# Attention over 16 images: three PSUM banks in one ring for the short products, one bank for the long ones

## The chip, the cores and the metric

The kernel runs on one core of a Trainium2 chip. The metric is the device time of one execution in microseconds (us). Five engines work side by side, each in the order of its own program, and wait for each other through semaphores: PE (TensorE, matrix products; its weight loads are listed as PEld), DVE (VectorE), ACT (ScalarE), POOL (GpSimd) and SP (SyncE, which starts the DMAs). Products land in PSUM, which has eight banks of 128 partitions x 512 floats.

## The reference, cut to what matters

```python
x = x + mamba_block(layernorm(x), ...)          # x: (16, 224, 512)
qh = split_heads(layernorm(x) @ Wq + bq)        # 16 heads of depth 32
kh = split_heads(ctx @ Wk + bk)                 # ctx: (16, 750, 512)
vh = split_heads(ctx @ Wv + bv)
logits = einsum('bhqd,bhkd->bhqk', qh, kh) / sqrt(32) + mask * -1e9
out = einsum('bhqk,bhkd->bhqd', softmax(logits), vh)
x = x + merge_heads(out) @ Wo + bo
x = x + (gelu(layernorm(x) @ sign(w1).T * alpha1 + b1)) @ sign(w2).T * alpha2 + b2
```

The second addition is the phase that the change touches.

## The kernel before, in words

Three phases follow each other: the scan (functions up to line 995, which also makes keys and values for the attention), the attention (`attention_phase`, line 998) and the feed-forward part (from about line 1690). The order of all work is written out by hand, as a loop over slots for each engine.

In the attention each image b has 16 slots. The 224 queries are two tiles of 112 rows; the 16 heads are four groups g of four heads; G = 4b + g counts groups over all images. A slot is half of the 750 keys for one tile of queries and one group. With `at` = slot - 16b, what stands in a slot on PE, in this order, is:

- `scores(n)` (line 1164): four products into the four banks of `sps`. They wait until DVE has read the four products of the slot before.
- `transpose_p(m, pair)` for m = slot - 3 and pair = 0, 1, 2 (line 1180): four transpositions each of exponentials into a bank of `tps`. I call them the first, second and third tile of the slot. ACT copies the first and the third to `pT` (line 1315), DVE the second (line 1434).
- then, in some slots, one or two of these: `project_q` (line 1150, at = -2, 1, 5, 9), `transpose_h` twice (line 1131, at = -3, which is slot 13 of the image before), `out_proj` (line 1214, in slots 6 and 7 of the next image), `weigh_v` in two halves (line 1204, in slots 3 and 4, 7 and 8, 11 and 12, 15 and 16) and `spread_sums` (line 1189, in slots 4, 8, 12 and 16). A slot 16 is slot 0 of the next image. Slots 2 and 10 have nothing behind the transpositions.

On DVE a slot is: `scale_o` in every fourth slot (line 1453, it reads a weighed product), four reductions of the scores (line 1420), in slot 10 `stats_of_x1` for the next image (line 1383), `invert_sums` every fourth slot, in slot 8 `row_stats`, in slot 11 `normalise`, then the copy of the second tile (line 1434), then `add_residual` (line 1459, reads an output projection). On ACT a slot is: a copy of a query, of `transpose_h` or of the sums, if there is one, then an exponential (line 1307), the copy of the first tile, an exponential, the copy of the third tile.

Two sets of two banks hold what PE makes besides the scores. `tps` takes the tiles in turn: tile number % 2, three tiles a slot. `ups` takes everything else in turn, by a counter in `take_bank`. Before PE writes into a bank it waits for the semaphore that says that the last content has been read. `pt_act` and `pt_dve` count the copies of tiles, `q32`, `hT`, `rb`, `oT` and `x2` the readings of the others.

Of the kernel before, what the change touches and what calls it, by code (L numbers as in the profile page):

```python
# [7 lines left out]
P = 128  # L8
# [5 lines left out]
BANK = 512  # L14
# [983 lines left out]
def attention_phase(nc, t, x1_dram, x2_dram, k_dram, v_dram, mv_dram, mv2, row_mv, wsum, ident, shared, early, sps):  # L998
# [11 lines left out]

    B, D, KEYS = t["ctxT"].shape
    L = x1_dram.shape[1]
# [11 lines left out]
    SCALE = float(DH) ** -0.5  # L1025
    N_ALL = B * SLOTS
    assert KC * CHUNKS == KEYS and CHUNKS % 2 == 0 and 2 * L <= BANK

    pe, act, dve, pool, sp = nc.tensor, nc.scalar, nc.vector, nc.gpsimd, nc.sync
    with ExitStack() as stack:  # L1030
# [65 lines left out]

        def pairs_of(tile):
            return tile // PAIRS, tile % PAIRS

        def place(m, pair):  # L1100
# [4 lines left out]
        def transposed(tile):  # L1105
            return tps[0:KC, tile % 2, 0:4 * TT].rearrange("p (c l) -> p c l", c=4)

        def tensor_program():
            freed = [None, None]
            count = [0]  # L1110

            def take_bank(unit, sem, value):

                bank = bank_of[unit] = count[0] % 2
                count[0] += 1
                if freed[bank] is not None:
                    pe.wait_ge(*freed[bank])
                freed[bank] = (S[sem], value)
                return bank
# [6 lines left out]
            def transpose_h(b, part):  # L1126
                bank = take_bank(("hT", b, part), "hT", 2 * (b - 1) + part + 1)
                pe.wait_ge(S["ln"], b)
                for k2 in range(2):
                    for i in range(2):  # L1130
                        mm = pe.transpose(ups[:, bank, k2 * L + i * TT:k2 * L + (i + 1) * TT],
                                          ln[:, i, (2 * part + k2) * P:(2 * part + k2 + 1) * P], ident[0:TT, 0:TT])
                signal(("hT", b, part), mm)

            def value_bias():

                bank = take_bank("bv", "bo", 1)
                pe.wait_ge(S["bv"], 1)
                for k in range(KD):
                    mm = pe.matmul(ups[0:TT, bank, :], bv_wide[:, k, :], wo[:, k, :],  # L1140
                                   start=(k == 0), stop=(k == KD - 1))
                signal("bv", mm)

            def project_q(b, g):
                G = b * GROUPS + g
                bank = take_bank(("q", G, 0), "q32", G + 1)
                if b:
                    pe.wait_ge(S["hT"], 2 * b)
                for k in range(KD):
                    mm = pe.matmul(ups[:, bank, 0:L], wq[:, k, g * P:(g + 1) * P], hT[:, k, :],  # L1150
                                   start=(k == 0), stop=(k == KD - 1))
                signal(("q", G, 0), mm)
# [15 lines left out]
            def transpose_p(m, pair):  # L1168

                tile = m * PAIRS + pair  # L1170
                pe.wait_ge(S["exp"], 2 * m + (1 if pair == 0 else 2))
                if tile >= 2:
                    n, before = pairs_of(tile - 2)
                    if before == 1:
                        pe.wait_ge(S["pt_dve"], n + 1)
                    else:
                        pe.wait_ge(S["pt_act"], 2 * n + before // 2 + 1)
                for c in range(4):
                    head, chunk = divmod(4 * pair + c, CHUNKS)
                    mm = pe.transpose(tps[0:KC, tile % 2, c * TT:(c + 1) * TT],  # L1180
                                      sc[buffer_of(m // 2)][:, 2 * (m % 2) + head, chunk * KC:(chunk + 1) * KC],
                                      ident[0:TT, 0:TT])
                mm.then_inc(S["t_ps"], 1)

            def spread_sums(G):
                bank = take_bank(("r", G, 0), "rb", G + 1)
                pe.wait_ge(S["rwide"], G + 1)
                for i in range(2):
                    mm = pe.matmul(ups[:, bank, i * TT:(i + 1) * TT], rwide[:, i].rearrange("p j d -> p (j d)"),
                                   ident[0:TT, 0:TT], start=True, stop=True)  # L1190
                signal(("r", G, 0), mm)

            def weigh_v(b, g, part):
                G = b * GROUPS + g
                if part == 0:
                    take_bank(("pv", G, 0), "oT", G + 1)
                    pe.wait_ge(S["pt_act"], 2 * GROUP * (G + 1))
                    pe.wait_ge(S["pt_dve"], GROUP * (G + 1))
                    if b:
                        pe.wait_ge(S[f"v{b % 2}"], 16 * loads(b))  # L1200
                bank = bank_of["pv", G, 0]
                for c in range(part * CHUNKS // 2, (part + 1) * CHUNKS // 2):
                    for j in range(GROUP):
                        mm = pe.matmul(ups[j * DH:(j + 1) * DH, bank, 0:L],
                                       v[b % 2][:, c, (g * GROUP + j) * DH:(g * GROUP + j + 1) * DH],
# [4 lines left out]
            def out_proj(b, i):  # L1210
                bank = take_bank(("o", b, i), "x2", 2 * b + i + 1)
                pe.wait_ge(S["oT"], GROUPS * (b + 1))
                for g in range(GROUPS):
                    mm = pe.matmul(ups[0:TT, bank, :], oT[b % 2][:, g, i * TT:(i + 1) * TT], wo[:, g, :],
                                   start=(g == 0), stop=(g == GROUPS - 1))
                signal(("o", b, i), mm)

            def spread_alpha():
# [3 lines left out]
                for k in range(KD):  # L1222
                    mm = pe.matmul(ups[:, bank, k * P:(k + 1) * P], ones[:], diag[:, k, :], start=True, stop=True)
                signal("alpha", mm)

            def transpose_rows(k):
                bank = take_bank(("rows", k), "rows_lo", k + 1)
                pe.wait_ge(S["rows"], 1)
                for i in range(4):
                    mm = pe.transpose(ups[:, bank, i * P:(i + 1) * P], rows[:, i, k * P:(k + 1) * P], ident[:])  # L1230
                signal(("rows", k), mm)
# [11 lines left out]
            for slot in slots:  # L1243
# [10 lines left out]
                for b in range(B):  # L1254
# [21 lines left out]
        def scalar_program():  # L1276

            def keep_hT(b, part):
                act.wait_ge(S["unit"], unit_of["hT", b, part])
                act.wait_ge(S["unit"], unit_of["q", b * GROUPS - 1, 0])  # L1280
                act.activation(hT[:, 2 * part:2 * part + 2, :],
                               ups[:, bank_of["hT", b, part], 0:2 * L].rearrange("p (k l) -> p k l", k=2),
                               ACT.Copy).then_inc(S["hT"], 1)
# [7 lines left out]
            def keep_q(G):  # L1291
                g = G % GROUPS
                act.wait_ge(S["unit"], unit_of["q", G, 0])
                if G >= 2:
                    act.wait_ge(S["s_ps"], GROUP * (G - 1))
                act.activation(q32[G % 2][:], ups[:, bank_of["q", G, 0], 0:L], ACT.Identity, bias=bq[:, g:g + 1],
                               scale=SCALE).then_inc(S["q32"], 1)
# [19 lines left out]
            def keep_sums(G):  # L1317
                act.wait_ge(S["unit"], unit_of["r", G, 0])
                if G:
                    act.wait_ge(S["oT"], G)  # L1320
                act.activation(rb[:], ups[:, bank_of["r", G, 0], 0:L], ACT.Copy).then_inc(S["rb"], 1)

# [14 lines left out]
            def keep_rows(k):  # L1337
                act.wait_ge(S["unit"], unit_of["rows", k])
                act.wait_ge(S["unit"], unit_of["q", B * GROUPS - 1, 0])
                act.activation(rowsT[0][:, k, :], ups[:, bank_of["rows", k], :], ACT.Copy).then_inc(S["rows_hi"], 1)  # L1340

# [36 lines left out]
        def vector_program(steps):  # L1378
# [27 lines left out]
            def fold_bv():  # L1406
                dve.wait_ge(S["unit"], unit_of["bv"])
                dve.wait_ge(S["bo_in"], 16)
                dve.tensor_tensor(bo[0:TT, :], bo[0:TT, :], ups[0:TT, bank_of["bv"], :], ALU.add).then_inc(S["bo"], 1)

# [36 lines left out]
            def scale_o(b, g):  # L1447
# [3 lines left out]
                if b >= 2:  # L1451
                    dve.wait_ge(S["unit"], unit_of["o", b - 2, 1])
                dve.tensor_tensor(oT[b % 2][:, g, :], ups[:, bank_of["pv", G, 0], 0:L], rb[:],
                                  ALU.mult).then_inc(S["oT"], 1)

            def add_residual(b, i):
                dve.wait_ge(S["unit"], unit_of["o", b, i])
                dve.wait_ge(S["res"], b + 1)
                dve.tensor_tensor(xt[b % 2][:, i, :], xt[b % 2][:, i, :], ups[0:TT, bank_of["o", b, i], :],
                                  ALU.add).then_inc(S["x2"], 1)  # L1460
# [24 lines left out]
            def keep_alpha():  # L1485
                dve.wait_ge(S["unit"], unit_of["alpha"])
                dve.tensor_copy(alpha2_row[:], ups[:, bank_of["alpha"], 0:D]).then_inc(S["alpha2_row"], 1)

# [9 lines left out]
            def split_rows(k):  # L1498
                dve.wait_ge(S["rows_hi"], k + 1)
                dve.wait_ge(S["unit"], unit_of["hT", B - 1, 1])  # L1500
                dve.wait_ge(S["xout0"], 16 * (B // 2))
                dve.tensor_tensor(rowsT[1][:, k, :], ups[:, bank_of["rows", k], :], rowsT[0][:, k, :].bitcast(F32),
                                  ALU.subtract).then_inc(S["rows_lo"], 1)

            for slot in slots:
# [508 lines left out]
```

## Time and profile before

| | us |
|---|---|
| median of 3 runs | 3625.31 (3621.59 to 3629.66) |
| the profiled execution, its time | 3627.49 |
| the profiled execution, its span | 3626.2 |
| attention, from its first product to the first that belongs to the feed-forward part (line 1239) | 1949.94 to 3185.2 |
| one image in the middle, mean of 14 | 75.84 |

The image's mean is taken from the first `out_proj` of image 0 (start 2049.59 us) to that of image 14 (start 3111.33 us): 1061.74 / 14. In a timeline the time from one `sps` row of line 1164 on PE to the next is the length of a slot. The rows of the timeline merge instructions that follow each other without a gap; a matrix product of 32-bit floats that is not a transposition is counted twice.

### The profile page before, as it was taken

How to read it: one execution, taken by the hardware profiler on the slowest of the kernel's cores; microseconds unless marked ns; L12 is line 12 of the kernel's file. 1: busy time of each engine (PE TensorE's matmuls, PEld its weight loads, DVE VectorE, ACT ScalarE, POOL GpSimd, SP SyncE).
4: the chain of work that ended last, by engine and by line, in shares of the span. 5: the costliest groups of instructions: out<-in, count | busy, mean ns of one | idle time of the engine just before them, and what ended most of it. 6: DMA issues, size and time to landing. Idle time of an engine off the chain costs nothing. (4 is left out here: it accounts for less than half of the span.)

```text
span 3626.2 us, 59832 instructions
## 1 busy us (share of the span) xinstructions
PE 3250.3 (90%) x20864; PEld 2243.3 (62%) x20864; DVE 2653.0 (73%) x4673; ACT 2401.2 (66%) x5339; POOL 1804.0 (50%) x1211
## 2 busy tenths in 40 slices
PE   5799988989889898889997899998999999899999
PEld 4566655666556665566554565555656556568887
DVE  2899999999999999999885666666666666532222
ACT  5778888787887878878753666666666666622222
POOL 2678888788887888788871000000000000045454
PEclk8899999999999999999999999999999999999999
DMA  5667766677666766576662111112111121111010
GB/s 165 161 175 195 188 171 168 162 197 188 169 156 175 194 186 167 154 186 175 176 184 94 54 60 45 46 52 80 49 46 45 53 78 52 50 52 47 24 47 23
DMA packets 286298, 425.03 MB, mean 117 GB/s; under 512 B 28753, under 2 KB 226129, under 8 KB 281394
## 3 DMA queue, kind: packets, MB, share of 16 engines
q1 hardware_dynamic: 278637, 411.44, 40.6%
q10 hardware_dynamic: 7365, 9.77, 0.9%
q8 instruction: 170, 2.79, 0.3%
q14 instruction: 126, 1.03, 0.1%
HBM read 320.12 MB, written 101.02 MB: 116 GB/s over the span
## 5 line engine op out<-in xcount | busy, mean ns | idle before, releaser
L811 POOL TENSOR_TENSOR a_hs<-a_rep,a_bmat 128x896 f32<-128x896 f32 x512 | 1061.4, 2097 | 287.7 <-PE a_yps L323 287.2
L443 ACT ACTIVATE a_states<-a_rep,a_a_neg 128x224 f32<-128x224 f32 x2048 | 793.6, 437 | 105.3 <-DVE a_hs L707 103.3
L700 DVE TENSOR_TENSOR_SCAN a_states<-a_states,a_hs 128x900 f32<-128x900 f32 x384 | 779.6, 2030 | 71.0 <-ACT a_states L443 56.4
L1420 DVE CUSTOM_DVE_ANT_0 b_sc<-sps,early_mask 112x375 f32<-112x375 f32 x1024 | 499.9, 545 | 230.8 <-PE sps L1164 218.1
L1180 PEld LDWEIGHTS b_tps<-ident,b_sc 112*125 112x125 f32 x3072 | 384.1, 192 | 281.7 <-issue 258.1
L1180 PE MATMUL b_tps<-ident,b_sc 112*125 112x112 f32 x3072 | 467.7, 290 | 100.7 <-ACT b_pT L1315 73.9
L1560 POOL TENSOR_SCALAR b_x_var<-mv 112x2 f32<-112x2 f32 x16 | 3.4, 213 | 946.1 <-DVE mv L1471 946.1
L1307 ACT ACTIVATE b_sc<-b_sc,b_nmax 112x750 f32<-112x750 f32 x512 | 466.7, 911 | 0.1
L1315 ACT ACTIVATE b_pT<-b_tps 125x448 f32<-125x448 f32 x512 | 277.6, 542 | 267.2 <-PE b_tps L1180 260.2
L345 PE MATMUL a_work<-early_scan_hT,w_in 128*128 128x224 f32 x2048 | 425.7, 363 | 9.4 <-issue 6.7
L707 DVE TENSOR_TENSOR a_hs<-a_states,a_cmat 128x896 f32<-128x896 f32 x384 | 419.1, 1091 | 13.2
L345 PEld LDWEIGHTS a_work<-early_scan_hT,w_in 128*128 128x128 f32 x2048 | 396.6, 196 | 49.5 <-issue 42.1
L400 PE MATMUL a_work<-ctx,a_wk 128*128 128x250 f32 x1536 | 348.6, 379 | 13.3 <-ACT kv_out L490 13.3
L404 PE MATMUL a_work<-wv,ctx 128*125 128x512 f32 x768 | 349.2, 597 | 9.9 <-ACT kv_out L487 9.3
L323 PE MATMUL a_yps<-a_hs,a_fold 128*32 128x224 f32 x4096 | 238.5, 375 | 114.6 <-POOL a_hs L818 46.0
L400 PEld LDWEIGHTS a_work<-ctx,a_wk 128*128 128x128 f32 x1536 | 289.5, 191 | 64.3 <-issue 17.2
L700 DVE TENSOR_TENSOR_SCAN a_hs<-a_states,a_hs 128x900 f32<-128x900 f32 x128 | 258.9, 2022 | 25.9 <-ACT a_states L443 25.9
L375 PE MATMUL a_work<-a_w_out,a_yT 128*112 128x512 f32 x512 | 249.8, 645 | 29.8 <-DVE early_du L690 29.7
L1813 ACT ACTIVATE c_g<-sps,early_b,early_alpha 128x512 f32<-128x512 f32 x112 | 87.1, 779 | 276.5 <-PE sps L1739 270.6
L323 PEld LDWEIGHTS a_yps<-a_hs,a_fold 128*32 128x32 f32 x4096 | 131.1, 114 | 224.0 <-DVE a_hs L707 102.6
L1849 DVE CAST c_gT_hi<-c_g 128x512 fp32r<-128x512 f32 x112 | 67.5, 603 | 274.2 <-ACT c_g L1813 274.2
L1887 POOL TENSOR_TENSOR c_gT_lo<-c_g,c_gT_hi 128x512 fp32r<-128x512 f32 x112 | 146.3, 1308 | 207.4 <-DVE c_gT_hi L1849 207.4
(199 smaller groups left out, 5020.5 us busy)
## 6 DMA issues: line engine op xcount, KB each, us to landing
a_rep<-du_scratch SPq DMA_DIRECT2D x512, 224.0 KB, 5.7
w_in<-W_in_dram SPq DMA_DIRECT2D x128, 512.0 KB, 4.4
du_scratch<-early_du SPq DMA_DIRECT2D x16, 1792.0 KB, 11.6
ctx<-ctxT_dram SPq DMA_DIRECT2D x48, 500.0 KB, 6.0
v_scratch<-kv_out SPq DMA_DIRECT2D x96, 250.0 KB
k_scratch<-kv_out SPq DMA_DIRECT2D x96, 250.0 KB, 4.5
b_keys<-k_scratch SPq DMA_DIRECT2D x8, 1500.0 KB, 8.8
b_v<-v_scratch SPq DMA_DIRECT2D x8, 1500.0 KB
```

The lines of the kernel that those rows point to most:

```text
L323: mm = pe.matmul(yps[j * DG:(j + 1) * DG, tile % 2 * L:(tile % 2 + 1) * L], fold[:], hs[(G4 * tile + j) % RING][:, q, 1:ROW], start=(q == ...
L345: mm = pe.matmul(work[:, bank, j * L:(j + 1) * L], w_in[unit % WINS][:, k, j * P:(j + 1) * P], hT[:, k, :], start=(k == 0), stop=(k == KD ...
L400: mm = pe.matmul(work[:, bank, j * WIDE:(j + 1) * WIDE], wk[:, k, (2 * half + j) * P:(2 * half + j + 1) * P], keys[:, k, :], start=(k == 0 ...
L404: mm = pe.matmul(work[0:KC, bank, :], keys[:, k, half * KC:(half + 1) * KC], wv[:, k, :], start=(k == 0), stop=(k == KD - 1))
L443: e = act.activation(rows(states[:, g % DA, :])[:, q, 1:ROW], rep[tile % REPS][:, j, 0, :], ACT.Exp, scale=a_neg[:, g % SLOTS, q:q + 1])
L700: dve.tensor_tensor_scan(state if g % G4 else whole, state, whole, 0.0, ALU.mult, ALU.add).then_inc(S["scan"], 1)
L707: dve.tensor_tensor(hh[:, :, 1:ROW], rows(states[:, g % DA, :])[:, :, 1:ROW], cmat[b % 2][:], ALU.mult).then_inc(S["hc"], 1)
L811: pool.tensor_tensor(hs[g % RING][:, :, 1:ROW], rep[tile % REPS][:, j, 1, :].unsqueeze(1).broadcast_to([P, Q, L]), bmat[b % 2][:], ALU.mul ...
L1180: mm = pe.transpose(tps[0:KC, tile % 2, c * TT:(c + 1) * TT], sc[buffer_of(m // 2)][:, 2 * (m % 2) + head, chunk * KC:(chunk + 1) * KC], i ...
L1307: act.activation(scores, scores, ACT.Exp, scale=-1.0, bias=nmax[:, block % 3, j:j + 1], accum_out=esum[:, block % 2, head:head + 1]).then_ ...
L1315: act.activation(place(m, pair), transposed(tile), ACT.Copy).then_inc(S["pt_act"], 1)
L1420: dve.tensor_tensor_reduce(out=sc[buffer_of(block)][:, j, cols], in0=sps[0:TT, j, 0:HALF], in1=mask[:, block % 2, cols], scale=-1.0, scala ...
```

## The change

The three banks `tps` now serve tiles, queries, `transpose_h`, the spread sums and the small products at the start and the end (`value_bias`, `spread_alpha`, `transpose_rows`), in the order in which PE issues them, with one counter. The one bank `ups` serves `weigh_v` and `out_proj` alone; `take_wide` makes each wait until the one before has been read. `out_proj` and `add_residual` come one slot earlier (slots 5 and 6 of the next image), and at the start DVE reads `spread_alpha` one slot and `value_bias` two slots earlier.

```diff
+    BANKS = 3
...
-        tps = mem.psum("tps", [P, 2, BANK])
-        ups = mem.psum("ups", [P, 2, BANK])
+        tps = mem.psum("tps", [P, BANKS, BANK])
+        ups = mem.psum("ups", [P, BANK])
...
         def transposed(tile):
-            return tps[0:KC, tile % 2, 0:4 * TT].rearrange("p (c l) -> p c l", c=4)
+            return tps[0:KC, bank_of["t", tile], 0:4 * TT].rearrange("p (c l) -> p c l", c=4)
...
-            freed = [None, None]
+            freed = [None] * BANKS
             count = [0]
+            wide = []
+
+            def take_wide(sem, value):
+
+                if wide:
+                    pe.wait_ge(*wide[-1])
+                wide.append((S[sem], value))
 
             def take_bank(unit, sem, value):
 
-                bank = bank_of[unit] = count[0] % 2
+                bank = bank_of[unit] = count[0] % BANKS
...
-                if tile >= 2:
-                    n, before = pairs_of(tile - 2)
-                    if before == 1:
-                        pe.wait_ge(S["pt_dve"], n + 1)
-                    else:
-                        pe.wait_ge(S["pt_act"], 2 * n + before // 2 + 1)
+                if pair == 1:
+                    bank = take_bank(("t", tile), "pt_dve", m + 1)
+                else:
+                    bank = take_bank(("t", tile), "pt_act", 2 * m + pair // 2 + 1)
...
                 if part == 0:
-                    take_bank(("pv", G, 0), "oT", G + 1)
+                    take_wide("oT", G + 1)
...
             def out_proj(b, i):
-                bank = take_bank(("o", b, i), "x2", 2 * b + i + 1)
+                take_wide("x2", 2 * b + i + 1)
...
-                    if at - SLOTS - 6 in range(2):
-                        out_proj(b, at - SLOTS - 6)
+                    if at - SLOTS - 5 in range(2):
+                        out_proj(b, at - SLOTS - 5)
...
-                if slot == 7:
+                if slot == 6:
                     keep_alpha()
-                if slot == 5:
+                if slot == 3:
                     fold_bv()
...
-                    if at - SLOTS - 6 in range(2):
-                        add_residual(b, at - SLOTS - 6)
+                    if at - SLOTS - 5 in range(2):
+                        add_residual(b, at - SLOTS - 5)
```

Where the order stands still and only the waits change, the listing of PE's instructions with the semaphores they wait for shows it. The semaphores' numbers are those of the scan phase reused, and the listing prints the scan's names: a_log_small is here `pt_dve`, a_const `pt_act`, a_rep2 `exp`, a_guess `rb`, a_xout3 `q32`, a_h `oT`, a_xin3 `ln`. PE in slot 13 of an image, the three tiles and the two transpositions of the next image's rows, before:

```order
L1180 MATMUL b_tps<-ident,b_sc 125x112 [waits a_log_small,a_rep2]
L1180 MATMUL b_tps<-ident,b_sc 125x112 x3
L1180 MATMUL b_tps<-ident,b_sc 125x112 [waits a_const,a_rep2]
L1180 MATMUL b_tps<-ident,b_sc 125x112 x3
L1180 MATMUL b_tps<-ident,b_sc 125x112 [waits a_const,a_rep2]
L1180 MATMUL b_tps<-ident,b_sc 125x112 x3
L1131 MATMUL b_ups<-ident,early_ln 128x112 [waits a_xin3,a_h]
L1131 MATMUL b_ups<-ident,early_ln 128x112 x3
L1131 MATMUL b_ups<-ident,early_ln 128x112 [waits a_xin3,a_guess]
L1131 MATMUL b_ups<-ident,early_ln 128x112 x3
```

The first tile waits for DVE's copy of the slot before, the second for ACT's third tile of the slot before, the third for ACT's copy of the first tile of its own slot. The same place now:

```order
L1185 MATMUL b_tps<-ident,b_sc 125x112 [waits a_log_small,a_rep2]
L1185 MATMUL b_tps<-ident,b_sc 125x112 x3
L1185 MATMUL b_tps<-ident,b_sc 125x112 [waits a_const,a_rep2]
L1185 MATMUL b_tps<-ident,b_sc 125x112 x3
L1185 MATMUL b_tps<-ident,b_sc 125x112 [waits a_guess,a_rep2]
L1185 MATMUL b_tps<-ident,b_sc 125x112 x3
L1138 MATMUL b_tps<-ident,early_ln 128x112 [waits a_xin3,a_const]
L1138 MATMUL b_tps<-ident,early_ln 128x112 x3
L1138 MATMUL b_tps<-ident,early_ln 128x112 [waits a_xin3,a_log_small]
L1138 MATMUL b_tps<-ident,early_ln 128x112 x3
```

The third tile now waits for the copy of the sums of slot 12, whose product had the bank; the second transposition of rows waits for DVE's copy of this slot's second tile. PE's tiles in slot 11 (behind a slot that has nothing but tiles), now; before they read as in the first piece:

```order
L1185 MATMUL b_tps<-ident,b_sc 125x112 [waits a_const,a_rep2]
L1185 MATMUL b_tps<-ident,b_sc 125x112 x3
L1185 MATMUL b_tps<-ident,b_sc 125x112 [waits a_log_small,a_rep2]
L1185 MATMUL b_tps<-ident,b_sc 125x112 x3
L1185 MATMUL b_tps<-ident,b_sc 125x112 [waits a_const,a_rep2]
L1185 MATMUL b_tps<-ident,b_sc 125x112 x3
L1208 MATMUL b_ups<-b_pT,b_v 32x224 [waits a_log_small,a_bc_stored,a_const,a_h]
```

Here the wait for DVE's copy of slot 10 has gone from the first tile to the second, and each tile waits for the same tile of the slot before.

## Rows read from the trace of the kernel before

**Rows 1.** The page, busy tenths of PE in 40 slices.

```profile
PE   5799988989889898889997899998999999899999
```

**Rows 2.** Windows: length, PE, PEld, DVE, ACT, POOL busy, PEclk, DMA share, GB/s.

```profile
2049.59:3111.33 1061.74, 969.24 (x8179) 631.46 (x8177) 698.01 (x2521) 700.05 (x1543) 62.58 (x168) 0.97 0.17 58
...
2609.00:2613.00 4.00, 3.94 (x36) 2.14 (x36) 2.09 (x6) 2.48 (x7) 2.25 (x6) 0.57 0.33 124
```

**Rows 3.** Tile view of b_tps, 2049.59 to 3111.33: idle before, us and times.

```profile
  ACT b_pT L1315: 62.9, 218
  DVE b_pT L1434: 22.6, 15
```

**Rows 4.** Timeline of PE, slots 9 to 11 of one image: start, length, line.

```profile
2558.39 0.90 PE L1164 MATMUL sps<-early_keys,b_q 32*112 32x375 f32 x8
2559.22 1.12 PE L1180 MATMUL b_tps<-ident,b_sc 112*125 112x112 f32 x8
2560.63 0.66 PE L1180 MATMUL b_tps<-ident,b_sc 112*125 112x112 f32 x4 [0.29 <-ACT b_pT L1315]
2561.13 1.69 PE L1150 MATMUL b_ups<-early_hT,early_wq 128*128 128x224 f32 x8
2562.75 0.90 PE L1164 MATMUL sps<-early_keys,b_q 32*112 32x375 f32 x8
2563.58 1.13 PE L1180 MATMUL b_tps<-ident,b_sc 112*125 112x112 f32 x8
2564.99 0.66 PE L1180 MATMUL b_tps<-ident,b_sc 112*125 112x112 f32 x4 [0.29 <-ACT b_pT L1315]
2565.82 0.90 PE L1164 MATMUL sps<-early_keys,b_q 32*112 32x375 f32 x8 [0.17 <-DVE b_half_min L1420]
...
2568.84 1.34 PE L1204 MATMUL b_ups<-b_pT,b_v 125*32 125x224 f32 x24
2570.11 0.90 PE L1164 MATMUL sps<-early_keys,b_q 32*112 32x375 f32 x8
```

**Rows 5.** Timeline, the tiles' weight loads in the first of these slots.

```profile
2559.22 0.95 PEld L1180 LDWEIGHTS b_tps<-ident,b_sc 112*125 112x125 f32 x8 [0.54 <-issue]
...
2560.60 0.51 PEld L1180 LDWEIGHTS b_tps<-ident,b_sc 112*125 112x125 f32 x4 [0.44 <-issue]
```

**Rows 6.** Timeline, ACT's copy of the first tile, DVE's first reduction.

```profile
2559.94 0.54 ACT L1315 ACTIVATE b_pT<-b_tps 125x448 f32<-125x448 f32 x1 [0.19 <-PE b_tps L1180]
...
2563.72 0.55 DVE L1420 CUSTOM_DVE_ANT_0 b_sc<-sps,early_mask 112x375 f32<-112x375 f32 x1 [1.66 <-PE sps L1164]
```

**Rows 7.** Timeline, slot 11 of an image and DVE's tail of slot 10.

```profile
2605.18 0.90 PE L1164 MATMUL sps<-early_keys,b_q 32*112 32x375 f32 x8 [0.17 <-DVE b_half_min L1420]
...
2605.46 1.28 DVE L1383 BATCH_NORM_STATS2 early_stats<-b_xt 112x6 f32<-112x512 f32 x2
...
2606.94 0.59 DVE L1434 COPY b_pT<-b_tps 125x448 f32<-125x448 f32 x1
...
2607.67 1.10 PE L1180 MATMUL b_tps<-ident,b_sc 112*125 112x112 f32 x8 [1.59 <-DVE b_pT L1434]
```

**Rows 8.** Timeline of PE, slot 13, up to the next slot's scores.

```profile
2541.59 0.90 PE L1164 MATMUL sps<-b_keys,b_q 32*112 32x375 f32 x8
...
2544.33 0.93 PE L1131 MATMUL b_ups<-ident,early_ln 112*128 112x112 f32 x8
2545.19 0.90 PE L1164 MATMUL sps<-b_keys,b_q 32*112 32x375 f32 x8
```

**Rows 9.** Timeline of DVE in the same slot: the copy of the second tile.

```profile
2544.63 0.62 DVE L1434 COPY b_pT<-b_tps 125x448 f32<-125x448 f32 x1
```

**Rows 10.** Timeline of PE: an output projection, and two places near the phase's end.

```profile
2588.21 3.60 PE L1214 MATMUL b_ups<-early_wo,b_oT 128*112 128x512 f32 x8
...
3154.62 0.66 PE L1180 MATMUL b_tps<-ident,b_sc 112*125 112x112 f32 x4 [2.02 <-ACT b_pT L1315]
...
3178.68 7.09 PE L1214 MATMUL b_ups<-early_wo,b_oT 128*112 128x512 f32 x16 [1.02 <-DVE b_oT L1453]
```

More of the change, by code:

```diff
@@ L1130, in transpose_h @@
                     for i in range(2):
-                        mm = pe.transpose(ups[:, bank, k2 * L + i * TT:k2 * L + (i + 1) * TT],
+                        mm = pe.transpose(tps[:, bank, k2 * L + i * TT:k2 * L + (i + 1) * TT],
                                           ln[:, i, (2 * part + k2) * P:(2 * part + k2 + 1) * P], ident[0:TT, 0:TT])
@@ L1139, in value_bias @@
                 for k in range(KD):
-                    mm = pe.matmul(ups[0:TT, bank, :], bv_wide[:, k, :], wo[:, k, :],
+                    mm = pe.matmul(tps[0:TT, bank, :], bv_wide[:, k, :], wo[:, k, :],
                                    start=(k == 0), stop=(k == KD - 1))
@@ L1149, in project_q @@
                 for k in range(KD):
-                    mm = pe.matmul(ups[:, bank, 0:L], wq[:, k, g * P:(g + 1) * P], hT[:, k, :],
+                    mm = pe.matmul(tps[:, bank, 0:L], wq[:, k, g * P:(g + 1) * P], hT[:, k, :],
                                    start=(k == 0), stop=(k == KD - 1))
@@ L1188, in spread_sums @@
                 for i in range(2):
-                    mm = pe.matmul(ups[:, bank, i * TT:(i + 1) * TT], rwide[:, i].rearrange("p j d -> p (j d)"),
+                    mm = pe.matmul(tps[:, bank, i * TT:(i + 1) * TT], rwide[:, i].rearrange("p j d -> p (j d)"),
                                    ident[0:TT, 0:TT], start=True, stop=True)
@@ L1200, in weigh_v @@
                         pe.wait_ge(S[f"v{b % 2}"], 16 * loads(b))
-                bank = bank_of["pv", G, 0]
                 for c in range(part * CHUNKS // 2, (part + 1) * CHUNKS // 2):
                     for j in range(GROUP):
-                        mm = pe.matmul(ups[j * DH:(j + 1) * DH, bank, 0:L],
+                        mm = pe.matmul(ups[j * DH:(j + 1) * DH, 0:L],
                                        v[b % 2][:, c, (g * GROUP + j) * DH:(g * GROUP + j + 1) * DH],
@@ L1210, in out_proj @@
             def out_proj(b, i):
-                bank = take_bank(("o", b, i), "x2", 2 * b + i + 1)
+                take_wide("x2", 2 * b + i + 1)
                 pe.wait_ge(S["oT"], GROUPS * (b + 1))
                 for g in range(GROUPS):
-                    mm = pe.matmul(ups[0:TT, bank, :], oT[b % 2][:, g, i * TT:(i + 1) * TT], wo[:, g, :],
+                    mm = pe.matmul(ups[0:TT, :], oT[b % 2][:, g, i * TT:(i + 1) * TT], wo[:, g, :],
                                    start=(g == 0), stop=(g == GROUPS - 1))
@@ L1222, in spread_alpha @@
                 for k in range(KD):
-                    mm = pe.matmul(ups[:, bank, k * P:(k + 1) * P], ones[:], diag[:, k, :], start=True, stop=True)
+                    mm = pe.matmul(tps[:, bank, k * P:(k + 1) * P], ones[:], diag[:, k, :], start=True, stop=True)
                 signal("alpha", mm)
@@ L1229, in transpose_rows @@
                 for i in range(4):
-                    mm = pe.transpose(ups[:, bank, i * P:(i + 1) * P], rows[:, i, k * P:(k + 1) * P], ident[:])
+                    mm = pe.transpose(tps[:, bank, i * P:(i + 1) * P], rows[:, i, k * P:(k + 1) * P], ident[:])
                 signal(("rows", k), mm)
@@ L1281, in keep_hT @@
                 act.activation(hT[:, 2 * part:2 * part + 2, :],
-                               ups[:, bank_of["hT", b, part], 0:2 * L].rearrange("p (k l) -> p k l", k=2),
+                               tps[:, bank_of["hT", b, part], 0:2 * L].rearrange("p (k l) -> p k l", k=2),
                                ACT.Copy).then_inc(S["hT"], 1)
@@ L1295, in keep_q @@
                     act.wait_ge(S["s_ps"], GROUP * (G - 1))
-                act.activation(q32[G % 2][:], ups[:, bank_of["q", G, 0], 0:L], ACT.Identity, bias=bq[:, g:g + 1],
+                act.activation(q32[G % 2][:], tps[:, bank_of["q", G, 0], 0:L], ACT.Identity, bias=bq[:, g:g + 1],
                                scale=SCALE).then_inc(S["q32"], 1)
@@ L1320, in keep_sums @@
                     act.wait_ge(S["oT"], G)
-                act.activation(rb[:], ups[:, bank_of["r", G, 0], 0:L], ACT.Copy).then_inc(S["rb"], 1)
+                act.activation(rb[:], tps[:, bank_of["r", G, 0], 0:L], ACT.Copy).then_inc(S["rb"], 1)
             def sign_w1(k, loaded):
@@ L1339, in keep_rows @@
                 act.wait_ge(S["unit"], unit_of["q", B * GROUPS - 1, 0])
-                act.activation(rowsT[0][:, k, :], ups[:, bank_of["rows", k], :], ACT.Copy).then_inc(S["rows_hi"], 1)
+                act.activation(rowsT[0][:, k, :], tps[:, bank_of["rows", k], :], ACT.Copy).then_inc(S["rows_hi"], 1)
             for slot in slots:
@@ L1501, in split_rows @@
                 dve.wait_ge(S["xout0"], 16 * (B // 2))
-                dve.tensor_tensor(rowsT[1][:, k, :], ups[:, bank_of["rows", k], :], rowsT[0][:, k, :].bitcast(F32),
+                dve.tensor_tensor(rowsT[1][:, k, :], tps[:, bank_of["rows", k], :], rowsT[0][:, k, :].bitcast(F32),
                                   ALU.subtract).then_inc(S["rows_lo"], 1)
```

12 lines of the change are left out of this document (5 added, 7 removed).

## The prediction

> **What bounds the kernel now.** I read the 40 slices of the page first: from slice 22 on, where the attention starts, PE is at 9 tenths nearly everywhere [rows 1]. The windows then say who else could be the bound: in the 1061.74 us of 14 images PE is busy 969 us, DVE 698, ACT 700, the DMA engines 17% [rows 2]. So PE's order is the bound, and what counts is where it stands still. The tile view names two waits: 62.9 us in 218 pieces for ACT's copy of a tile, and 22.6 us in 15 pieces for DVE's copy [rows 3]. The first is one 0.29 us gap a slot (14 images have 224 slots), the second about one an image.
>
> The timeline shows both. In a usual slot the scores take 0.83 us until the tiles start, the first two tiles run together, then the third waits for ACT, then the next product follows [rows 4]. Tile loads follow each other at (0.95 - 0.19) / 7 = 0.109 us where nothing waits (0.19 being one load), and the third tile's load starts 2560.60 - 2559.22 = 1.38 us after the first tile's, where eight loads need 0.87 [rows 5]. So the wait costs 0.51 us a slot, not the 0.29 that the idle column says, since a product's tail is counted as busy.
>
> A slot with nothing behind its tiles is not bound by this: 2562.75 to 2565.82 is 3.07 us, and the scores that end it wait for DVE. DVE starts to reduce 0.97 us after the scores start [rows 6] and needs four reductions of 0.47 and 0.2 of signalling. This loop of 3.07 us stays as it is.
>
> **The change part by part.** I write slot times from the start of its scores. Lengths of slots 0 to 15 in the trace, read as in [rows 4], are 4.73, 4.36, 3.07, 4.29, 4.73, 4.36, 6.27, 7.54, 4.74, 4.36, 3.07, slot 11, slot 12, 3.60, 4.36, 4.10; slots 11 and 12 contain the clock's fall and would without it be 5.70 (the tiles start at 2.46, the weighing 1.97 later, as in slots with no fall, and lasts 1.27) and 4.73, together 74.0 us. The measured mean is 75.84, so the clock costs 1.8 an image.
>
> Third tile. It no longer waits for a copy of its own slot. Its bank was last held by the third tile of the slot before, or by a query or the sums made there, which ACT copies first thing in the slot, ending some 0.6 us in; the tile is due at 1.7. ACT is free for it: 700 of 1062 us busy [rows 2]. Twelve slots (all but 2, 10, 11, 13) have other PE work behind the tiles and are over the 3.07 loop, so they shorten by 0.50 each: 6.0 us.
>
> What stands behind the tiles. A query, the spread sums or a row transposition now takes the bank of this slot's first tile. ACT's copy of it starts 0.72 us after the tiles start and lasts 0.54 [rows 6]; with the 0.12 of signalling it frees the bank at 1.38. A query is due at 12 x 0.109 = 1.31, so it waits 0.07, in three slots an image (1, 9, 14); behind weighed values or an output projection the bank is long free. -0.2.
>
> Slot 11. DVE's copy of slot 10's second tile stands behind the statistics (1.28 us) and ends at 2607.53, 2.35 us into slot 11; the tiles wait for it till 2.49 [rows 7]. Now only the second tile waits for it: the first runs inside the wait. From 2.46 come eight transpositions (0.87), 0.19 until the weighing, which is 1.27 long [rows 4]: 4.7 to 4.8 us against 5.70. +1.0. The row scale that DVE needs for `normalise` starts earlier as well, since ACT's copy of the first tile is 1.6 us earlier, so that DVE's copy in slot 11 ends near 6.0; slot 12's second tile waits for it 0.1. -0.1. The cover is thin here: each further 0.1 us on DVE in slot 11 goes to PE.
>
> Slot 13. The second row transposition takes the bank of this slot's second tile, so it waits for DVE's copy: that ends at 2544.63 + 0.62, 3.66 us into the slot [rows 8, 9]. It starts at 3.75 and takes half of 0.86, so slot 14 starts at 4.18 instead of 3.60: -0.6 where other slots give 0.5. Behind the waiting transposition PE has slot 14's scores, and DVE waits for these, idle for 1.5 us. In slot 14 ACT has the second half of the rows to copy (0.5 us) before its exponential, so that the first tile's bank and the query behind it are 0.2 late. -0.2.
>
> Slot 3. Today its first tile waits 0.2 for DVE's copy in slot 2; now the second tile does, and it is due later. +0.2.
>
> Output projections, one slot earlier. They are 3.53 us of PE each [rows 10] wherever they stand. In slot 5 the first follows `scale_o`, which DVE ends 1.0 us into the slot, 1.1 before the projection is due. The second waits for `add_residual` (0.69 us) of the first, and between them stand a query, scores and tiles, 4 us. The weighing of slot 7 waits for the second `add_residual`: scores and tiles, 2.2 us, cover its 0.8. Cost 0, and if the covers were gone up to 0.8 an image.
>
> Sum without the clock: 6.0 - 0.2 + 1.0 - 0.1 - 0.6 - 0.2 + 0.2 = 6.1 us an image, 74.0 to 67.9.
>
> The clock. The granted clock falls to half (1.2 GHz) in 14 of the 15 images that have the statistics in slot 10, right behind the 1.59 us wait of slot 11: 0.57 on the mean of 2609 to 2613 [rows 2, 7]. Elsewhere, with waits of 0.3 us in every slot, it stays at 2.4 GHz (0.97 in the mean of 14 images [rows 2]). In the changed kernel the longest wait there is 2.46 - 1.27 = 1.2 us, though the slot before now has 0.8 idle in one piece (tiles end at 2.3, scores wait till 3.07). The bounds are no fall at all (cost 0) and the fall of today (1.8). I take the middle, 0.9: a gain of 0.9, 7.0 an image.
>
> By the Trainium skill, "TensorE: Matmul & The Clock Gate", section "A second HAM failure mode: psum-queue depth-cycling", a kernel that cycles through PSUM banks each iteration can make PE idle so often that its clock swings between the two levels, at a cost. Trusted fully, it would have the clock fall at the new waits too, and the sum would be rival A's. The trace of before agrees only in part: 0.29 us in every slot from a cycle of two banks left the clock at 2.4 GHz.
>
> Start and end. Up to the first output projection the gains are one image's: slots 5, 7 to 15 and 0 to 4 less the slots without other work, 7. Behind image 14's first projection: slots 6 to 9, 2.0. At the end the third tile waits 2.02 us for ACT while ACT takes a sign of the weights [rows 10], and DVE's reductions of the same slot wait for that tile because only two score buffers are left; with a bank of its own it is early, but ACT's copies follow soon as the bound. I take +5 of 0 to 8. The last two output projections run back to back today (7.09 us [rows 10]); with one bank the second waits for the first's `add_residual`: 0.69 and twice 0.1: -0.9. The reading of `value_bias` and `spread_alpha` moves inside covered time: 0.
>
> 14 x 7.0 + 7 + 2 + 5 - 0.9 = 111 us. The profiled execution took 3627.5, so 3516.5; the median is 2.2 lower, so 3514.
>
> **The rivals.** A: the clock falls twice an image, in slot 11 and at the 1.0 us wait of slot 13. Two falls cost 3.6 instead of 1.8: 6.1 - 1.8 = 4.3 an image, 65 over 15, some 70 in all, 3555. For it: two new waits near each other, and 0.8 idle in slots 2 and 10. Against it: single waits of 0.3, and several together, have not done it.
>
> B: the third tile's gain is half lost, because the exponentials become the bound. A tile needs the exponential that ACT ends 2.2 us after the tiles of the slot before; PE comes faster now, and ACT waits 0.19 before its first copy where sums precede it [rows 6]. If ACT fell back by 0.25 in each slot, 3 us an image would be left, with the clock's 0.9 some 3565. Against it: ACT's work is 2.8 us in slots of 3.5 and more.
>
> C: slower. In the eight slots behind a query or the sums the first tile waits for DVE's copy of the slot before, as all do today; `scale_o`, `row_stats` and the faster PE push that copy back. It ends at 3.7 us after the scores of its slot start and would be needed at 3.85 + 0.83 = 4.68: a margin of 1.0. It decides if the copy is 1.8 late; at 2.0, each of the eight loses 1.0 and gains 0.5, 4 lost against some 2 won elsewhere, 2 an image: 3655. Against it: DVE is idle a third of the time [rows 2].
>
> D: the change doesn't do what it says: the third tile's bank is free but the tile is issued no earlier. The eight transpositions across two banks at 0.109 speak against it [rows 5]. Then only slot 11's 1.0 and slot 13's loss stay: about 3620.
>
> **How the numbers follow.** Forecast 0.65, at 3514, A 0.15, B 0.13, C 0.03, D 0.04. The forecast's own range, from the clock's bounds (0.9 x 15 = 14 each way) and the end's, is 3498 to 3533. For 8 in 10 the range goes from 3495 to 3558, which takes in A. A measurement of this kernel can tell 0.2% (7 us) from no change: faster holds the forecast, A, B and nearly half of D, 0.95; same 0.02; slower 0.03.
>
> **What would show it.** Right: twelve transpositions in one row of PE's timeline, 1.3 us from first start to the next product, in all slots but 11; the wait for ACT b_pT before tiles near 0; a wait of about 1.2 us for DVE b_pT once in an image in slot 11, before the second tile, and one of 1.0 before L1138; slots 2 and 10 still 3.07; a mean image of 68.8. A clock row at 0.57 in every image would cost the 0.9, two would be A. Wrong: rows of four transpositions with a wait for ACT in front, slots with a query over 4.0 us, or slots 2 and 10 over 3.1.

## The result and the profile after

The changed kernel takes 3512.43 us (median of 4 runs, 3508.16 to 3518.84), the kernel before 3627.48 beside it. The ratio is 0.9683, 95% interval 0.9657 to 0.9709. The forecast was 3514. The profiled execution has a span of 3514.3 us against 3626.2.

Where the time went can be read from four marks that both traces have: the attention's first product, the first output projection of images 0 and 14, and the first product of line 1239 (after: 1243).

| us | before | after | gain | forecast |
|---|---|---|---|---|
| start of the attention | 1949.94 | 1956.52 | -6.6 | 0 |
| an image, mean of 14 | 75.84 | 68.30 | 7.54 | 7.0 |
| 14 images | 1061.7 | 956.1 | 105.6 | 98 |
| attention, whole | 1235.3 | 1117.6 | 117.7 | 111 |
| from there to the end of the span | 441.0 | 440.2 | 0.8 | 0 |

The start is later by 6.6 us though nothing of the scan was changed. In another profiled execution of the changed kernel (run `after_again` below) the attention starts at 1948.51, so this is the scan's own spread. The forecast of 111 us for the attention was 6.7 short, and the late scan hid that in the total: that the time meets the forecast within 2 us is in part luck.

The page's PE line of after, to be held against [rows 1], and the windows of its 14 images, the answer to [rows 2] (columns as there):

```profile
PE   5699889888889888988998899999999999899999
```

```profile
2045.37:3001.50 956.13, 908.84 (x8178) 611.01 (x8177) 695.73 (x2523) 696.20 (x1543) 63.11 (x168) 0.99 0.19 64
...
2414.50:2417.90 3.40, 3.40 (x33) 1.80 (x36) 2.73 (x10) 1.83 (x5) 1.51 (x4) 0.53 0.29 95
```

The same instructions (8178 products) now fill 956 us instead of 1062. PE's busy time fell too, 969 to 909, because its products' tails overlap more (twelve transpositions in one row are busy for 1.56 us, eight and four apart for 1.12 + 0.66 = 1.78) and because the clock is higher: 0.99 in the mean instead of 0.97. DVE and ACT do what they did. The second row is one of the stretches in which the clock is still down, at 0.53 with PE busy throughout.

The tile view of the same stretch, the answer to [rows 3] (tps now holds the row transpositions and queries too):

```profile
  DVE b_pT L1438: 43.4, 43
  ACT b_sc L1311: 26.6, 49
  ACT b_pT L1319: 21.0, 57
...
  PEld b_tps L1194: 19.7, 55
...
  PE b_tps L1185: 14.3, 16
```

The last two lines are of the view's second part, which says who waited. ACT's copy was waited for 218 times and is now 57 times, of which 55 (19.7 us) are the weight loads of the spread sums. These loads stood idle for as long before (20.1 us in 56 pieces, put down to `issue`), so that nothing is lost there. DVE's copy has become the longer wait: of the 14.3 us that PE stood ahead of tiles 13.7 are in slot 11 (14 x 0.98), and 13.3 more are ahead of the second row transposition of slot 13, which its weight loads count a second time.

PE's timeline, a slot with a query and then slots 10 to 13 of one image, to be held against [rows 4, 7, 8]:

```profile
2437.93 0.90 PE L1171 MATMUL sps<-b_keys,b_q 32*112 32x375 f32 x8
2438.76 1.56 PE L1185 MATMUL b_tps<-ident,b_sc 112*125 112x112 f32 x12
2440.16 1.70 PE L1157 MATMUL b_tps<-early_hT,early_wq 128*128 128x224 f32 x8
2441.79 0.90 PE L1171 MATMUL sps<-b_keys,b_q 32*112 32x375 f32 x8
...
2477.39 0.90 PE L1171 MATMUL sps<-b_keys,b_q 32*112 32x375 f32 x8
...
2480.46 0.90 PE L1171 MATMUL sps<-b_keys,b_q 32*112 32x375 f32 x8 [0.68 <-DVE b_half_min L1424]
2481.29 0.69 PE L1185 MATMUL b_tps<-ident,b_sc 112*125 112x112 f32 x4
2482.96 1.10 PE L1185 MATMUL b_tps<-ident,b_sc 112*125 112x112 f32 x8 [0.98 <-DVE b_pT L1438]
2483.99 1.34 PE L1208 MATMUL b_ups<-b_pT,b_v 125*32 125x224 f32 x24
2485.26 0.90 PE L1171 MATMUL sps<-b_keys,b_q 32*112 32x375 f32 x8
...
2489.48 0.90 PE L1171 MATMUL sps<-b_keys,b_q 32*112 32x375 f32 x8
...
2491.71 0.55 PE L1138 MATMUL b_tps<-ident,early_ln 112*128 112x112 f32 x4
2493.20 0.60 PE L1138 MATMUL b_tps<-ident,early_ln 112*128 112x112 f32 x4 [0.95 <-DVE b_pT L1438]
2493.74 0.90 PE L1171 MATMUL sps<-b_keys,b_q 32*112 32x375 f32 x8
```

Twelve transpositions stand in one row. The query follows 1.40 us after the first of them (it was 1.91), and its slot is 3.86 instead of 4.36. Slot 10 is still 3.07. Slot 11 has the first tile ahead of the wait and is 4.80. Slot 13 has the new wait of 0.95 and is 4.26, longer than the 3.60 of before. At the end of the phase:

```profile
3047.20 0.66 PE L1234 MATMUL b_tps<-ident,early_rows 128*128 128x128 f32 x4 [1.65 <-ACT b_pT L1319]
...
3066.56 3.66 PE L1218 MATMUL b_ups<-early_wo,b_oT 128*112 128x512 f32 x8 [1.02 <-DVE b_oT L1457]
3071.00 3.69 PE L1218 MATMUL b_ups<-early_wo,b_oT 128*112 128x512 f32 x8 [0.78 <-DVE b_xt L1463]
```

The wait for ACT, which takes a sign of the weights there, has moved from the third tile to the rows behind the tiles [rows 10], and the last two projections stand 4.44 us apart instead of 3.53.

### The profile page after: what moved, and what is told of

Same layout as the page of the kernel before. It is cut to its first block and busy times, and to the rows that moved or that the text cites. A ratio compares the mean times of both kernels' runs of the same rounds, so it can differ in the third digit from the quotient of the medians.

```text
span 3514.3 us, 59833 instructions
## 1 busy us (share of the span) xinstructions
PE 3186.9 (91%) x20864; PEld 2223.5 (63%) x20864; DVE 2650.7 (75%) x4673; ACT 2396.1 (68%) x5339; POOL 1805.3 (51%) x1211
## 5 line engine op out<-in xcount | busy, mean ns | idle before, releaser
L1185 PEld LDWEIGHTS b_tps<-ident,b_sc 112*125 112x125 f32 x3072 | 362.2, 191 | 157.4 <-issue 126.1
L1185 PE MATMUL b_tps<-ident,b_sc 112*125 112x112 f32 x3072 | 410.7, 283 | 16.3 <-DVE b_pT L1438 14.9
```

Of the source, the lines that this page charges most:

```text
L1185: mm = pe.transpose(tps[0:KC, bank, c * TT:(c + 1) * TT], sc[buffer_of(m // 2)][:, 2 * (m % 2) + head, chunk * KC:(chunk + 1) * KC], ident ...
```

## The experiments

Times are medians; "mean image" is measured between the first projections of images 0 and 14. "Quiet image" is the length that most images have in which the clock does not fall; in `before` and `move_only` one image of the 14 is such. Falls are the stretches at half clock that begin between those two marks, counted in the trace's granted clock.

| kernel | us | ratio to before, 95% | mean image | quiet image | falls |
|---|---|---|---|---|---|
| before | 3630 | | 75.84 | 74.40 | 13 |
| changed | 3512 | 0.9683 (0.9657 to 0.9709) | 68.30 | 67.49 | 6 |
| changed, again | 3508 | 0.9668 (0.9649 to 0.9687) | 68.29 | 67.49 | 5 |
| `move_only` | 3629 | 0.9998 (0.9987 to 1.0008) | 75.81 | 74.40 | 13 |
| `ring_only` | 3513 | 0.9678 (0.9662 to 0.9693) | 68.60 | 68.37 | 1 |
| `third_waits` | 3610 | 0.9947 (0.9933 to 0.9962) | 74.49 | 73.58 | 5 |
| `first_waits` | 3531 | 0.9726 (0.9712 to 0.9741) | 69.73 | 68.97 | 10 |
| `stats_late` | 3500 | 0.9643 (0.9629 to 0.9657) | 67.57 | 67.44 | 0 |
| `h_split` | 3506 | 0.9655 (0.9641 to 0.9670) | 67.96 | 66.84 | 7 |
| `both` | 3485 | 0.9605 (0.9584 to 0.9626) | 66.91 | 66.78 | 0 |
| `both`, again | 3489 | 0.9611 (0.9595 to 0.9627) | 66.92 | 66.79 | 0 |
| `all_late` | 3484 | 0.9598 (0.9583 to 0.9612) | 66.53 | 66.40 | 0 |

The changed kernel was run a second time, as the base of the later experiments:

> The changed kernel once more, as the reference for the three others on this chip: 3512, within 6 us.

Its quiet image is again 67.49, its falls 5 instead of 6, and its median 4 us lower.

**The two halves of the change.** `move_only` is the kernel before with this alone:

```diff
-                    if at - SLOTS - 6 in range(2):
-                        out_proj(b, at - SLOTS - 6)
+                    if at - SLOTS - 5 in range(2):
+                        out_proj(b, at - SLOTS - 5)
...
-                    if at - SLOTS - 6 in range(2):
-                        add_residual(b, at - SLOTS - 6)
+                    if at - SLOTS - 5 in range(2):
+                        add_residual(b, at - SLOTS - 5)
```

> The kernel before, with its two pairs of banks, and only the output projections and the additions of the residual one slot earlier. Theory (the gain is the bank ring's): PE's work and its waits are the same, the 3.53 us of a projection stand in slots 5 and 6 instead of 6 and 7, so 3627 us, within 6 us. Rival (part of the gain is the move's, since the weighing of slot 7 no longer stands behind a projection): some 1 us an image, 3611.

3629 against 3630: the move gives nothing by itself. `ring_only` is the changed kernel with the same lines taken back.

> The changed kernel with the output projections left in slots 6 and 7. The weighing of slot 7 now stands right behind the second projection and needs its only bank. Theory: it waits for the addition of the residual, 0.9 us as between the last two projections of the trace after (4.44 us from start to start instead of 3.53), 15 or 16 times: 3512 + 14 = 3526. Rival (the wait is hidden, as the move was not needed): 3512.

Its time is that of the changed kernel, which is what the rival said, but for another reason. The wait is there, in DVE's and PE's timeline behind the second projection:

```profile
2465.88 0.69 DVE L1463 TENSOR_TENSOR early_xt<-early_xt,b_ups 112x512 f32<-112x512 f32 x1 [2.20 <-PE b_ups L1218]
...
2466.62 1.34 PE L1208 MATMUL b_ups<-b_pT,b_v 125*32 125x224 f32 x24 [0.78 <-DVE early_xt L1463]
```

It is 0.78 of idle and makes a quiet image 68.37 - 67.49 = 0.88 longer, as the theory had it; 14 of them are 12 us. But the clock fell once instead of six times. A fall costs 1.6 us (images of 69.1 beside 67.5 in the changed kernel), so five fewer give 8 back. The attention as a whole took 1121.2 us against 1117.6, and 1115.7 in the changed kernel's second run. What the two ways differ by in the total is below what the runs can tell.

**The third tile's wait**, put back alone:

```diff
                     bank = take_bank(("t", tile), "pt_act", 2 * m + pair // 2 + 1)
+                if pair == 2:
+                    pe.wait_ge(S["pt_act"], 2 * m + 1)
```

> The changed kernel, where the third tile of a slot waits again for ACT's copy of the first tile of its own slot, though it doesn't need that bank. Theory (this one wait is most of the gain): 0.43 to 0.50 us in twelve slots of an image, 5.8 an image, 89 over the phase: 3601. In slot 11 nothing, since the copy is done long before. Rival (the gain came from the ring as a whole, the clock and slot 11): under half of it, 3550 or less.

```profile
3091.89 0.90 PE L1171 MATMUL sps<-b_keys,b_q 32*112 32x375 f32 x8
3092.72 1.12 PE L1187 MATMUL b_tps<-ident,b_sc 112*125 112x112 f32 x8
3094.13 0.66 PE L1187 MATMUL b_tps<-ident,b_sc 112*125 112x112 f32 x4 [0.29 <-ACT b_pT L1321]
```

These are the rows of before again. 98 of the 115 us are gone, 9 more than expected. A quiet image is 73.58, so the wait is worth 6.09 us an image where 5.8 was expected. The rest is at the phase's end, where I had counted 2: from image 14's first projection to line 1239's product it takes 79.5 us instead of 72.6.

**The first tile's wait**, put back alone (`if pair == 0 and m: pe.wait_ge(S["pt_dve"], m)` at the same place).

> The changed kernel, where the first tile of every slot waits again for DVE's copy in the slot before. Theory: it matters in slot 11 alone, where four transpositions (0.44 us) go back behind the wait, and the wait is 1.6 us long again, so that the clock falls in nearly each image instead of 6 times in 15 (1.9 us a fall): 0.44 x 15 + 9 x 1.9 = 24 us, 3536, with 12 to 15 stretches at half clock. Rival (the clock doesn't hang on the length of this wait): 6.6 us, 3519, 6 stretches.

3531 lies between the theory's 3536 and the rival's 3519. PE's timeline in an image without a fall, slots 11 and 12, and DVE's scaling in between:

```profile
2419.61 0.90 PE L1171 MATMUL sps<-early_keys,b_q 32*112 32x375 f32 x8 [0.69 <-DVE b_half_min L1426]
2422.11 1.53 PE L1187 MATMUL b_tps<-ident,b_sc 112*125 112x112 f32 x12 [1.60 <-DVE b_pT L1440]
2423.57 1.34 PE L1210 MATMUL b_ups<-b_pT,early_v 125*32 125x224 f32 x24
2424.84 0.90 PE L1171 MATMUL sps<-early_keys,b_q 32*112 32x375 f32 x8
2424.87 1.00 DVE L1404 TENSOR_SCALAR early_ln<-b_xt,early_mv,early_rstd 112x512 f32<-112x512 f32 x2 [0.85 <-POOL early_rstd L128]
2426.56 1.53 PE L1187 MATMUL b_tps<-ident,b_sc 112*125 112x112 f32 x12 [0.81 <-DVE b_pT L1440]
```

Slot 11 is 5.23, 0.43 more, as expected. But slot 12 has a second wait, 0.81 us, that the theory left out: DVE's copy of slot 11 stands behind `normalise`, whose scale comes from ACT behind the copy of the first tile, and then from POOL. With the first tile late everything in that chain is: DVE stands idle for 0.85 us before it can scale. With 0.19 in slot 3 a quiet image is 1.48 longer. The falls went from 5 or 6 to 10, not to 14: there were more of them with the longer wait, and a long wait alone doesn't decide. Most of them cost little: an image with a fall takes 69.7 us beside 68.97, since slot 11 is then longer (up to 6.83 instead of 5.23) but slot 12 loses its wait (down to 4.22 instead of 5.08). The 1.48 us of waits, 21 us in 14 images, make all of the 18, and the further falls added nothing: the theory's sum came near by an error on each side.

**The two waits that are left.** `stats_late` calls `stats_of_x1` after `keep_pT` in DVE's slot:

```diff
-                    if at == -6 and b:
-                        stats_of_x1(b)
...
                 if before:
                     keep_pT(slot - 3)
                 for b in range(B):
                     at = slot - b * SLOTS
+                    if at == -6 and b:
+                        stats_of_x1(b)
```

> The changed kernel, with DVE's statistics of the next image's rows behind its copy of slot 10's second tile instead of ahead of it. Theory: the copy is done 1.5 us earlier and the 0.98 us wait in slot 11 goes; slot 11 is then held by DVE's reductions, which start 1.3 us late, so slot 12 starts at 4.3 instead of 4.8: 0.5 us an image, and fewer falls of the clock (6 of 1.9 us, if none is left 11 us): 3494 to 3505. Rival (the wait only moves to the end of slot 11 whole, as DVE is the bound there): 3512.

The time is in the expected range, yet half of the theory is wrong. PE's timeline from slot 11, and DVE's in between:

```profile
2470.66 0.90 PE L1171 MATMUL sps<-b_keys,b_q 32*112 32x375 f32 x8 [0.68 <-DVE b_half_min L1424]
...
2471.49 1.56 PE L1185 MATMUL b_tps<-ident,b_sc 112*125 112x112 f32 x12
...
2475.02 0.90 PE L1171 MATMUL sps<-b_keys,b_q 32*112 32x375 f32 x8 [0.70 <-DVE b_half_min L1424]
2475.02 1.00 DVE L1402 TENSOR_SCALAR early_ln<-early_xt,early_mv,early_rstd 112x512 f32<-112x512 f32 x2
...
2475.94 0.62 DVE L1438 COPY b_pT<-b_tps 125x448 f32<-125x448 f32 x1
...
2476.70 1.09 PE L1185 MATMUL b_tps<-ident,b_sc 112*125 112x112 f32 x8 [0.17 <-DVE b_pT L1438]
```

Slot 11 lost its 0.98 us wait inside and has one of 0.70 at its end; it is 4.36 instead of 4.80, but slot 12 is 4.61 instead of 4.22, because its second tile waits for the copy behind the scaling. A quiet image is 67.44, 0.05 better. What was gained is the clock: no fall at all.

`h_split` puts the second half of the row transpositions ahead of slot 14's tiles, and its copy on ACT behind that slot's first exponential:

```diff
+                if slot % SLOTS == SLOTS - 2 and 0 < slot < LAST:
+                    transpose_h(slot // SLOTS + 1, 1)
                 if before:
                     for pair in range(PAIRS):
                         transpose_p(slot - 3, pair)
...
                         transpose_h(b, 0)
-                        transpose_h(b, 1)
...
                         keep_hT(b, 0)
-                        keep_hT(b, 1)
...
                     exponential(2 * slot - 4)
+                if slot % SLOTS == SLOTS - 2 and 0 < slot < LAST:
+                    keep_hT(slot // SLOTS + 1, 1)
```

> The changed kernel, with the second half of the row transpositions ahead of slot 14's tiles instead of behind slot 13's, and its copy on ACT between slot 14's exponential and the copy of the first tile. Theory: the 0.95 us wait of slot 13 goes; slot 13 becomes 3.1 us (the loop over DVE), slot 14 takes 0.45 more and 0.1 of a late copy: together 7.5 instead of 8.1 us, 0.6 an image, 3503. Rival (ACT is late in slot 14 and the query waits for it as long as was won): 3512 or more.

```profile
2483.85 0.90 PE L1171 MATMUL sps<-b_keys,b_q 32*112 32x375 f32 x8
...
2486.92 0.90 PE L1171 MATMUL sps<-b_keys,b_q 32*112 32x375 f32 x8 [0.30 <-DVE b_half_min L1426]
2487.75 0.60 PE L1138 MATMUL b_tps<-ident,early_ln 112*128 112x112 f32 x4
...
2491.31 0.90 PE L1171 MATMUL sps<-b_keys,b_q 32*112 32x375 f32 x8
```

Slots 13 and 14 are 3.07 and 4.39, 7.46 instead of 8.12, and a quiet image is 66.84: the theory's 0.6. The total gained 2.4 us against the run of the changed kernel on the same chip, where 9 were due. Seven falls instead of five, and longer ones, took 4.6 of the 9: the 14 images are 4.5 us shorter in the traces, and the attention as a whole 5.9, but the scan ended 2.4 later in this run's trace.

> The two edits together. Theory: they act in different slots and add up: 3487 to 3497. Rival (the wait in slot 11 or 13 has the clock fall elsewhere): no better than the better of the two.

3485 is better than the range. The slots add up (a quiet image 66.78 with h_split's 0.66 in it), and no image has a fall. The times don't add: 8 and 2 us apart, 24 together. The totals overstate this, as the scan, which no edit touches, ends at a different time in each trace. The attention as a whole, from its first product to that of line 1243, is 1115.7 us in the changed kernel's second run, 1107.3 in `stats_late`, 1109.7 in `h_split` and 1097.4 in `both`: 8.3 and 5.9 apart, 18.2 together. The 4.0 beyond the sum fit the clock: the falls of `h_split` cost 4.6 more than those of the changed kernel, and where the statistics stand behind the copy there are none.

> The kernel of run `both`, with DVE's scaling of the next image's rows (1.0 us, in slot 11) also behind its copy of the second tile. Theory: the copy of slot 11 was what slot 12's second tile waited for; with the copy first, slot 12 goes from 4.61 to 4.22 us, 0.4 an image, 6 us: 3479. Rival (DVE's chain of copy, scaling and slot 12's reductions is the bound, so the wait moves to slot 13's scores): 3485, as `both`.

> The kernel of run `both` once more, as the reference on this chip: 3485, within 5 us, and again no stretch at half clock between the images' projections.

The second run of `both` has a quiet image of 66.79 and no fall again, and an attention of 1097.5 us. `all_late` moves `normalise` behind the copy as well. A quiet image is 66.40 against 66.79, slot 12 is 4.22: 0.39 as expected. In time it is 3483.7 against 3489.2 for `both` on the same chip, 5.5 us, with intervals that overlap; the attention is 1090.4 us against 1097.5. It has the shortest attention of the study and is 0.9% under the changed kernel by the ratios 0.9598 and 0.9683.

## Why the prediction was right

**The sum.** One image of before has no fall of the clock and takes 74.40 us, where the prediction added up 74.0; so the falls cost at most 1.4 an image there, not 1.8. From 74.40 to a quiet 67.49 are 6.9 us where 6.1 were forecast. A mean image is 1.44 us longer than a quiet one before and 0.81 after, nearly all of it the clock's, so the clock gave 0.6 where 0.9 was forecast. The two errors took part of each other away: 7.5 in all for 7.0.

**PE's order was the bound and 0.29 us of idle were worth 0.5.** Shown by `third_waits`. The reading of weight loads in [rows 5] gave 0.50 a slot; the timeline of after has 0.50 in a slot with a query and 6.09 / 12 = 0.51 in the mean.

**Slots 2 and 10 stay at 3.07.** So they are, at 0.68 us of idle now, waiting for DVE.

**The query waits 0.07 for the first tile's copy.** It doesn't. It follows 1.40 us after the tiles start, but so does the output projection (2460.78 to 2462.18), which needs no bank of the ring. The 1.31 is the distance of the weight loads, and the product starts 0.1 after its load. The 0.2 an image put down for this was nothing.

**Slot 11** was forecast at 4.7 to 4.8 and is 4.80.

**Slot 12** was the largest miss: its second tile was to wait 0.1 and waits for nothing, and in the quiet image of before the slot is 5.08, not the 4.73 of the prediction, so it gained 0.86 where 0.4 was forecast. `first_waits` shows why: the first tile being early also starts `normalise` early, without which slot 12 is again 5.08. In that image of before the slot begins so:

```profile
2459.70 0.90 PE L1164 MATMUL sps<-early_keys,b_q 32*112 32x375 f32 x8
2460.91 1.10 PE L1180 MATMUL b_tps<-ident,b_sc 112*125 112x112 f32 x8 [0.30 <-DVE b_pT L1434]
```

**Slot 13** was forecast at 4.18 and is 4.26, with a wait of 0.95 for DVE's copy where 1.0 was forecast. **Slot 14** was to lose 0.2 and lost nothing (3.86): ACT was done with the rows' second half sooner than I reckoned. Slots 5 to 7 together are 16.62, where 18.17 - 1.5 gives 16.67. With the 0.2 of the queries, the 0.2 of slot 14 and the 0.1 of slot 12 that did not come, a quiet image is 67.5 instead of 67.9.

**The output projections' covers held**: slots 5 and 6 with the projections and slot 7 with the weighing behind them are 7.27, 5.76 and 3.59 with no wait. `ring_only` shows that the cover of the weighing is what the move buys, 0.88 an image.

**The clock.** I took the middle of two bounds, 0.9 us an image. There were 6 falls of 1.6 us in 14 images, 0.7. That the middle was near is luck: the changed kernel's own two traces have 6 and 5, and nothing in the prediction gave that number. Rival A, a fall at each of two waits, did not come: the wait of slot 13 drew none by itself. Two pairs of banks had 13 falls in 14 images, the ring of three has 5 or 6, and the same ring with the statistics behind the copy has none.

**Rivals B, C and D** did not come either. The twelve slots are 0.50 to 0.52 shorter than in `third_waits`, so the exponentials do not bound them, and PE waits for DVE's copy ahead of tiles in 15 places in 14 images, not in eight slots of each.

The Trainium skill (page "TensorE: Matmul & The Clock Gate", section "A second HAM failure mode: psum-queue depth-cycling") describes a kernel with bf16 products of 512 columns whose cycling through banks each iteration leaves PE small idles, at which the clock swings. Here both orders cycle through banks, and with one and the same ring the falls go from 6 to none: the cycling alone does not bring a fall.

**Start and end.** The start gave 6.5 (7 forecast) and the end 5.6 (6.1 forecast), both with the differing slot order taken into account; the 0.9 for the last two projections is 0.91.

What stays open is what decides whether the clock falls. `ring_only` has the same waits in slots 10 and 11 as the changed kernel (0.68 and 0.98), and 1 fall instead of 5 or 6. Even within the changed kernel the length of the waits does not decide. This is slot 11 of an image with a fall; the one at 2480.46 above has the same two waits and none:

```profile
2411.36 0.90 PE L1171 MATMUL sps<-early_keys,b_q 32*112 32x375 f32 x8 [0.69 <-DVE b_half_min L1424]
...
2413.86 1.59 PE L1185 MATMUL b_tps<-ident,b_sc 112*125 112x112 f32 x8 [0.98 <-DVE b_pT L1438]
```

All 15 images that have the statistics have these two waits, to 0.01 us, in both traces of the changed kernel; 11 of the 30 have a fall, each beginning 2.3 to 3.0 us after the scores of slot 11. With the second wait gone from the inside of slot 11 (`stats_late`, `both`, `all_late`) no image has a fall, so it has a part in them; what picks the images is open.

## What to carry to other kernels

Where an engine's stream is the bound, a short wait for a buffer that the same step has just filled is worth more than its idle time in the profile: measure from start to start, of the weight loads where there are any. When banks go into one ring, go through the order and write down for each user who held its bank last and where on the reader's engine that reading stands; the reading that stands last (here DVE's copy behind statistics) sets the next wait. Work on the reader that nobody waits for soon belongs behind the copy that frees a bank.

## What the hardware showed that I had not expected

Two edits that were worth 8 and 2 us apart were worth 24 together, of which the attention as a whole shows 8.3, 5.9 and 18.2. The granted clock's falls (0 to 13 of them in 14 images) come and go with small shifts of PE's waits, and a fall has no fixed price: 1.6 us in the changed kernel, 3.1 where it lasted longer, 0.7 in `first_waits`, 0.8 to 2.5 in the kernel before. A change of 0.88 us an image (`ring_only`) could not be seen in the time at all for this reason. Between kernels that differ by under 1% here, the length of a quiet image and that of the attention say more than the total, which has the scan's spread in it (1946.84 to 1956.52 us until the attention starts).
